# A one-layer decoder on one core: late SiLUs and biases moved into the last stage's fill, the opening re-ordered

## The reference, cut to what matters

```python
x = _layernorm(x + _L0_attn_ref(x, w_project, w_out))          # 16 heads of 16, causal
x = _layernorm(x + _L0_xattn_ref(x, ctx, Wq, bq, ..., bo))     # 8 heads of 8, rotary
x = _layernorm(x + _L0_ffn_ref(x, w1, b1, ln_g, ln_b, w2, b2))
# _L0_ffn_ref, with bitlinear158 = act_quant(rms_norm(x)) @ weight_quant(w).T + b
h = silu(bitlinear158(x, w1, b1))        # 256 -> 1024
h = gelu(h, approximate=False)
h = layer_norm(h, ln_g, ln_b)
return bitlinear158(h, w2, b2)           # 1024 -> 256
# rms_norm: x * rsqrt(mean(x*x) + 1e-5); act_quant: scale = 127 / max(max|x|, 1e-5) of each row
```

## Time and profile before

| | us |
|---|---|
| median of 3 runs | 517.94 |
| the three runs | 517.68, 519.66, 517.94 |
| the profiled execution, its own time | 520.89 |
| its span | 519.1 |
| busy: PE, DVE, ACT, POOL | 462.3, 427.4, 358.7, 308.3 |

### The profile page before, as it was taken

One profiled execution on the slowest core, in us unless ns is written; L12 is line 12 of the kernel. 1 busy time (PEld: TensorE's weight loads), 2 busy tenths in 40 slices (PEclk: granted clock), 3 DMA queues, 4 the chain that ended last, 5 costly groups with the idle time before them and its releaser, 6 DMA issues. The chain is left out here.

```text
span 519.1 us, 12269 instructions
## 1 busy us (share of the span) xinstructions
PE 462.3 (89%) x4294; PEld 245.2 (47%) x4294; DVE 427.4 (82%) x892; ACT 358.7 (69%) x689; POOL 308.3 (59%) x457
## 2 busy tenths in 40 slices
PE   6787889999999999999999999988998785977786
PEld 4454545455455455545545454543433232544453
DVE  2856687989889898798999999898786869799993
ACT  2232266678687786777878776676787876899973
POOL 6744556465474754657455677767453218688873
PEclk9998699999999999999999999999899897899999
DMA  7132323252442523324252332321100000000001
GB/s 225 32 90 73 93 57 102 59 159 63 121 128 68 147 63 99 114 59 147 60 141 69 105 101 62 102 58 54 32 3 1 0 1 2 10 29 24 32 30 42
DMA packets 52460, 37.07 MB, mean 71 GB/s; under 512 B 21552, under 2 KB 47792, under 8 KB 52400
## 3 DMA queue, kind: packets, MB, share of 16 engines
q1 hardware_dynamic: 52112, 36.06, 24.3%
q10 hardware_dynamic: 288, 0.23, 0.2%
HBM read 24.48 MB, written 10.49 MB: 67 GB/s over the span
## 5 line engine op out<-in xcount | busy, mean ns | idle before, releaser
L893 ACT ACTIVATE PB<-e_b 128x512 f32<-128x512 f32 x256 | 148.2, 592 | 59.9 <-PE e_b L690 58.8
L1087 DVE TENSOR_REDUCE MX<-mx_b 128x2 f32<-128x512 f32 x256 | 166.8, 679 | 26.2 <-PE mx_b L662 24.8
L662 PE MATMUL mx_b<-KA,QA 48*128 48x256 bf16 x512 | 98.5, 279 | 11.2 <-DVE MX L1087 10.7
L690 PE MATMUL e_b<-QA,KA 50*128 50x256 bf16 x512 | 97.5, 275 | 0.5 <-ACT PB L893 0.4
L707 PE MATMUL u_b<-PB,VA 128*32 128x256 f32 x1024 | 84.4, 393 | 2.1 <-ACT PB L893 1.7
L662 PEld LDWEIGHTS mx_b<-KA,QA 48*128 48x128 bf16 x512 | 29.7, 94 | 87.3 <-issue 48.3
L1014 POOL TENSOR_TENSOR SP<-SP,srec 128x1024 f32<-128x1024 f32 x15 | 28.5, 1901 | 68.2 <-DVE srec L1059 68.2
L1004 POOL TENSOR_TENSOR KM<-QK,att_tab 128x512 f32<-128x512 f32 x31 | 32.0, 1052 | 21.5 <-ACT QK L847 21.5
L567 PE MATMUL g_b<-XT,wp 128*128 128x128 f32 x256 | 34.5, 290 | 4.9 <-DMA wp<-in_wpT 4.9
L707 PEld LDWEIGHTS u_b<-PB,VA 128*32 128x32 f32 x1024 | 22.4, 108 | 31.2 <-ACT PB L893 16.8
L567 PEld LDWEIGHTS g_b<-XT,wp 128*128 128x128 f32 x256 | 31.5, 200 | 8.1 <-DMA wp<-in_wpT 4.9
(11 more groups left out here) (204 smaller groups left out, 1105.4 us busy)
## 6 DMA issues: line engine op xcount, KB each, us to landing
KA<-parts_k SPq DMA_DIRECT2D x64, 96.0 KB
QA<-parts_q SPq DMA_DIRECT2D x64, 96.0 KB
parts_q<-part_q SPq DMA_DIRECT2D x32, 128.0 KB, 1.9
parts_k<-part_k SPq DMA_DIRECT2D x16, 192.0 KB, 2.1
C<-in_ctx SPq DMA_DIRECT2D x16, 128.0 KB, 3.5
X<-in_x SPq DMA_DIRECT2D x16, 128.0 KB, 2.8
out_y<-O SPq DMA_DIRECT2D x16, 128.0 KB, 1.7
XT<-in_xT SPq DMA_DIRECT2D x15, 128.0 KB, 2.1
```

The source lines that it names most:

```text
L662: m = nc.tensor.matmul(mx_b[n % 2][:, D * k:D * k + D], QA[low:low + K_MAX, 2 * i.ring + b, h, P * u:P * u + P], KA[low:low + K_MAX, 2 * i ...
L690: m = nc.tensor.matmul(e_b[n % 2][:, D * k:D * k + D], KA[low:low + K_EXP, 2 * i.ring + b, h, P * sc:P * sc + P], QA[low:low + K_EXP, 2 * ...
L893: nc.scalar.activation(PB[:, n % 4].rearrange("p e t -> p (e t)"), e_b[n % 2][:, :], ACT.Exp, scale=XC ** -0.5).then_inc(e_sb.sem, 1)
L1087: nc.vector.tensor_reduce(MX[:, b, e, 2 * q:2 * q + 2, u], mx_b[n % 2][:, :].rearrange("p (e s) -> p e s", e=2), AXL.X, ALU.max).then_inc( ...
```

## The change

In the **opening** the first queries are split on GpSimd and no longer on VectorE; the second pair's scaling `self_norm` goes the other way; one pair of constant-row fills is put at VectorE's very start and one behind the second pair's norm on GpSimd; ScalarE copies the second pair's values ahead of its exponentials. In turn -1 the third pair's self-attention stands 4 steps earlier (sum at step 4, transposes at 8, value product at 9, projection at 11), and ten idle products are spread through it; eleven before it are taken out.

In the **last block** the SiLUs of pairs 12 to 15 and the biases of pairs 14 and 15 move behind the first GELUs (GELU of pairs 0 to 3 in one run, then a table load, SiLU 12, later SiLU 13 to 15, and a load back), the last pair's second norm is applied by GpSimd, the last two pairs have one group of factors and one batch, and GpSimd's upper product of the first pairs stands behind the roots as it did for the later ones.

```diff
-        GROUPS = (slice(0, NPAIR - 4), slice(NPAIR - 4, NPAIR - 2), slice(NPAIR - 2, NPAIR - 1), slice(NPAIR - 1, NPAIR))
-        BATCHES = (slice(0, 4), slice(4, 8), slice(8, 12), slice(12, 14), slice(14, 15), slice(15, 16))
+        GROUPS = (slice(0, NPAIR - 4), slice(NPAIR - 4, NPAIR - 2), slice(NPAIR - 2, NPAIR))
+        BATCHES = (slice(0, 4), slice(4, 8), slice(8, 12), slice(12, 14), slice(14, 16))
...
@@ TensorE, body and prologue
-                    if s == 12 and real(a):
+                    if s == (12 if i.v >= 0 else 8) and real(a):
                         transpose_p(a)
-                    if s == 13 and real(a):
+                    if s == (13 if i.v >= 0 else 9) and real(a):
                         self_pv(a)
...
-                    if s == 15 and real(a):
+                    if s == (15 if i.v >= 0 else 11) and real(a):
                         out_proj(a)
+                    if i.v < 0:
+                        idle_products({2: 1, 3: 1, 4: 1, 6: 2, 10: 1, 13: 1, 14: 1, 15: 1}.get(s, 0))
...
                 v_proj(p1, mx_b[0])
-                idle_products(4)
                 rotary_proj("q", mx_b[1], p0)
                 rotary_proj("k", e_b[1], p1)
                 qk_proj(p2, g_b[2])
-                idle_products(12)
+                idle_products(5)
                 transpose_p(p1)
@@ ScalarE, prologue and body
+                v_copy(p1, mx_b[0])
                 self_exp(p1, 1)
                 self_exp(p1, 0)
-                v_copy(p1, mx_b[0])
...
+                    if i.v < 0 and s == 8:
+                        pt_copy(a)
+                        ao_copy(a)
...
@@ VectorE
+            ones_rows(nc.vector, 1)
             dve.wait_ge(ld_att, 16)
...
-                    if s == 9 and real(a):
+                    if s == (9 if i.v >= 0 else 4) and real(a):
                         self_sum(a)
...
-                    if s == 6 and i.v in (NPAIR - 3, NPAIR - 1):
-                        factors(dve, i.v // (NPAIR - 1))
+                    if s in (5, 6, 7, 8) and i.v in (NPAIR - 3, NPAIR - 1):
+                        factor(dve, i.v // (NPAIR - 1), s - 5)
...
-                ones_rows(nc.vector, 1)
                 norm1_stats(p0)
...
                 rotate("q", mx_b[1], p0)
-                split_parts(dve, nc.vector, "q", p0)
                 self_sum(p1)
+                self_norm(dve, nc.vector, p1)
                 rotate("k", e_b[1], p1)
@@ GpSimd, prologue and body
-                wait(pool, km[1], p1, 1)
-                ones_rows(nc.gpsimd, 2)
-                pool.wait_ge(s_pad[2], 2)
                 rstd(pool, ln1, p0, mv1, rs1)
-                self_norm(pool, nc.gpsimd, p1)
+                split_parts(pool, nc.gpsimd, "q", p0)
...
+                if i.v < 0:
+                    wait(pool, ln1, j, 6)
+                    ones_rows(nc.gpsimd, 2)
+                    pool.wait_ge(s_pad[2], 2)
+                    self_norm(pool, nc.gpsimd, a)
                 if real(j):
                     split_parts(pool, nc.gpsimd, "q", j)
...
@@ last block, ScalarE
+        LATE, AHEAD_G = NPAIR - 4, 4
...
-            for v in range(NPAIR):
+            for v in range(LATE):
                 first_value(v)
...
-                if v == 4:
-                    norm2(act, last)
+                if v == 3:
                     square_sum(act, last)
-                if v == 7:
+                if v == 9:
                     numbers_copy(act, 4, t_b[1])
-                if v == 11:
-                    numbers_copy(act, 5, t_b[0])
+
+            for v in range(AHEAD_G):
+                second_value(Pair(0, v))
             for t in range(TURNS2):
                 second_values(t)
+                if t == 2:
+                    first_value(LATE)
+                if t == 3:
+                    for v in range(LATE + 1, NPAIR):
+                        first_value(v)
@@ last block, GpSimd
-                if i and t < FILL:
-                    upper_product(i)
...
-                if i and i.v != NPAIR - 1 and t >= FILL:
+                if i and i.v != NPAIR - 1:
                     upper_product(i)
...
-            mean_power(pool, 2)
             add_row(pool, 12)
             add_row(pool, 13)
             rstd(pool, ln2, last, mv2, rs2)
+            wait(pool, ln2, last, 6)
+            nc.gpsimd.tensor_scalar(XALL[:, last.v, :], Y2[:], rs2[:, 1:2], rs2[:, 2:3], ALU.mult, ALU.add).then_inc(ln2.sem, 1)
+            mean_power(pool, 2)
             quantise(pool, 14)
-            mean_power(pool, 3)
+            quantise(pool, 15)
...
@@ last block, TensorE
                 if i and i.v == 0:
+                    idle_sums(7, 0)
+                if i and i.v in (1, 2):
+
+                    pe.wait_ge(f_sb, f_done(NPAIR - 3 + i.v))
...
@@ last block, VectorE
-            for v in range(EARLY, NPAIR):
+            for v in range(EARLY, NPAIR - 2):
                 first_bias(v)
...
             for t in range(TURNS2):
                 (turn if t < DRAIN else drain)(t)
+                if t in (1, 2):
+
+                    first_bias(NPAIR - 3 + t)
```

More of the change, by code:

```diff
@@ L734, in early_product, with idle_products @@
                 m.then_inc(f_ps.sem, 1)
+            def idle_products(n):
+                for _ in range(n):
+                    nc.tensor.matmul(u_b[:, :], identb[:], maskb[:].rearrange("p h s -> p (h s)"), start=True, stop=True)
             pe.wait_ge(ld_wp, 16)
@@ L792, in body @@
                             pv_quad(i, m)
-            def idle_products(n):
-                for _ in range(n):
-                    nc.tensor.matmul(u_b[:, :], identb[:], maskb[:].rearrange("p h s -> p (h s)"), start=True, stop=True)
             def prologue():
@@ L1381, in second_values @@
                                          scale=root[:, (i.v + LAG_G) % 4, 0:1]).then_inc(zs.sem, 1)
-                if i := pair_at(t, 0):
-                    wait(act, silu, i, 1)
-                    nc.scalar.activation(row_h(i), row_h(i), ACT.Gelu).then_inc(gelu.sem, 1)
+                if (i := pair_at(t, 0)) and i.v >= AHEAD_G:
+                    second_value(i)
                 if j:
```

64 lines of the change are left out of this document (33 added, 31 removed).

## The result

The changed kernel took **506.27 us** (median, 504.90 to 512.86), the kernel before 518.48 beside it: ratio 0.9745, 95% interval [0.9719, 0.9771]. The forecast was 507.0. Six executions (one here, two of e1, one each of e6, e7 and e12) are over 1.5% longer than the fastest of their kernel: they count in the medians, but not in the ratios, the intervals and the clock means.

A forecast was written before the change was run, and what follows sets the result against it. Attention turns were taken as throughput-bound (TensorE 20.6 of 21.0 us), gains lying in the opening and last stage's start. -3.1 - 2.8 + 0.9 - 6.0 = -11.0 from 520.89, less 2.95, gave 506.9, said as 507.0; range 503.6 to 512.5.

The forecast's parts named there:

- Term 1: Opening: first maximum product moves from 44.07 to 41.0, set by the first queries' expansion; -3.1 us (bounds -4.3 and -1.5).
- Term 2: First maximum to first exponential product: 15.6 us instead of 18.41, VectorE's 12.7 the floor; -2.8 us (bounds 0 and -5.7).
- Term 3: First turn: second queries' expansion lands late (0.6) and third pair's norm starts later (0.3); +0.9 us (bounds 0 and +3).
- Term 4: Last stage's fill: first GELU 5.8 earlier, first square 6.4, third square 6.0 at low clock; -6.0 us (bounds -4 and -6.9).
- Rival 1: Opening gives almost nothing: terms two and three cancel and half of the first stays; 511.4 us, chance 0.2.
- Rival 2: Last stage: ScalarE pauses 1.3 us around each extra table load, all behind 2.6 late; 509.5 us, chance 0.1.
- Rival 3: Slower: fewer idle products, TensorE's clock stays low into the first turns; one whole low turn gives 527.5 us, chance 0.05.

The follow-up runs named there:

- e1: Kernel before with only the opening and turn -1 part of the change, last stage as before: 515.32 us, ratio 0.9931.
- e2: Kernel before with only the factors' groups and last-stage part of the change, opening as before: 512.19 us, ratio 0.9878.
- e6: Changed kernel with the four factor steps together at step 6 of turns 13 and 15, as before: 511.63 us, ratio 0.9785.
- e7: The changed kernel, unaltered, measured again beside the experiments: 509.74 us, ratio 0.9809.
- e12: Changed kernel with GpSimd's upper product ahead of the roots again in the last stage's first four turns: 509.87 us, ratio 0.9814.
- e10: Changed kernel with the first queries' split on VectorE again and the second pair's norm on GpSimd: 510.21 us, ratio 0.9845.
- e5: Changed kernel plus seven idle products before the first maximum product and idle sums before the second and third row sums: 505.66 us, ratio 0.9752.
- e9: e5 plus idle products in turn 13 and ahead of pairs 8, 10 and 11 in the last stage: 506.57 us, ratio 0.9763.
- e3: Changed kernel with the late SiLUs and biases ahead of the first GELU again, without the two extra table loads: 512.41 us, ratio 0.9893.
- e11: Changed kernel with pair 15's SiLU moved behind turn 6 of the last stage, adding two table loads: 513.37 us, ratio 0.9900.

## Why the prediction was right, and where not

**The number.** 507.0 was forecast, 506.27 and 509.74 were measured, the first 0.7 under it and the second 2.7 over. The range (503.6 to 512.5) held both. The nearness is in part luck. In the two profiles the gain was 15.05 us where the terms had 11.0; subtracting the 2.95 by which the profiled execution stood above its median made up for most of what the terms lacked, and the two medians of one kernel lie 3.5 us apart. The range's lower end, too, was not built from the terms' stated better ends: with -5.7 and 0 for terms 2 and 3, in place of -3.6 and +0.5, it is 501.0.

**Two readings of the rows.** The turn of 21.0 us was a window's width: from one copy of US to the next it is 21.91 us in both profiles for most turns. Nothing in the sum hung on it. And the page of before has an 8 in the slice from 363 to 376 us that the prediction passed over: it is the fall in turn 14 told below.

**Term 1 (-3.1; measured -3.28; by e10's profile 1.4 to 2.2 of it is the split's move).** The chain came as written: norm at 24.65 (25.4), sum at 27.48 (28.3), transposes at 30.30 (31.6), first maximum product at 40.79 (41.0), with TensorE waiting for the expanded queries. One split operation beside VectorE's scaling took 1.64 us, as in the earlier trace rows. The 1.3 us by which the transposes were early did not help, since the transfer decided: the step that took the transfer's distances from before is the one that carried the number. It did so with two errors that cancel: the split ended at 32.28 and not 33.1, and the queries landed 6.1 us behind the issue (34.68 to 40.79) and not 5.5 (34.87 to about 40.4 before). Over the profiles of this opening the product comes at 40.18 to 41.51.

**Term 2 (-2.8; -3.22 in the profile).** The placing gave 14.8 us at full clock; 14.38 was measured three times (e1, e5, e9). At low clock I had 16.5, and 17.7 to 20.7 were measured at 0.59 to 0.71. The mistake was to take VectorE's 12.7 us as the floor at any clock and to price the idle products as harmless: in e6, at 0.59, TensorE is busy 20.02 of 20.69 us and is itself the bound. Even the bound of 0 did not hold: that stretch is 2.3 us longer than before. That -3.22 came near -2.8 is a matter of which execution was profiled.

**Term 3 (+0.9; +0.27 in the profile, +0.9 in e5, +3.7 in e9).** The mechanism is the one named, the second queries' expansion landing late, where there is a wait to see: 0.69 us in e5, 2.10 in e9. In the changed kernel's own profiles, and in e6's, TensorE does not wait for it at all, and where their 0.27 comes from was not traced.

**Term 4 (-6.0; -7.63, by the medians of e2 -6.3).** First GELU -6.5 (from the stage's start; -5.8 forecast), first square -7.1 (-6.4), third -7.6 (-6.0). The first 0.7 us come from the first GELU, and e1 shows that they need not be an error of the placing: in the profile of before that GELU stands at 23.73, in e1, with the same last block and no fall of the clock in front, at 22.43. Against e1 the change brings it 5.2 us forward, less than forecast. The rest is the third row product: it started 0.8 us earlier and, though it ran at low clock as forecast (3.63 us), the path behind it was 0.8 us shorter than I had it. e3 shows that the late SiLUs and biases are most of this term (4.4 us by the ratios, with an error of 2.7; 6.4 of 7.6 at the third square). The interval of e2 is 3.6 to 9.1 us.

**What the sum lacked.** Turns 13 and 14, priced at nothing, gave 1.70 us in the profile: 0.55 from turn 13 and 1.15 from a fall of the clock that the profile of before had and that of after not. The second is an accident of the two executions profiled, since e7, the same kernel, has a larger fall there.

**How much is the clock.** The fit's constants, the time with no clock lost, are 511.5 for before and 503.7 and 505.4 for the two measurements of the changed kernel: 6 to 8 us are work and waiting. The clock lost went from 12.2 to 3.5 and 6.1 us, worth 5.3 and 3.7 us by the slope. I had treated the clock as a detail of two terms; by the fit it is four tenths of the gain, and about a third with the six long executions kept in. The fit is a correlation; what ties it to a cause is e5's filled gap in front of the first maximum product.

**The rivals.** Rival 1 (opening worth little, 511.4) lies outside e1's interval, though e1's 3.6 us stand between its 0.6 and my 5.0, and with the two longest executions in, the mean gain of 1.9 us is nearer to the rival. Rival 2 (a drain at each load) is refuted by the rows of e11: the Trainium skill, ScalarE: Activation LUTs, section "What ACT_TABLE_LOAD costs", has 1.38 us of drain, and no load here had one. Rival 3 (the clock falls and eats the gain) has half of its mechanism shown: falls of 3.5 to 17 us happen in the changed opening, but the kernel before has one of 13.7 too, and none reached far into the turns in a profile. It is not ruled out for single executions: one of e1's twelve, at a clock of 0.951, took 527.36 us, 8 more than the median of before. No profile shows where it lost its 25.7 us of clock.

## What to carry over

Where one execution's profile is compared with another's, compare the granted clock by place first: here 12 us of full clock were lost on average, in three or four stretches that come and go. Many of them follow idle times of TensorE of 1.2 to 3.4 us, but not all: the 13.7 us in the opening of before follow one of 0.95, and e1's 10.5 us near 366 one of 0.66. Idle products placed exactly where TensorE stands (here seven in front of a late transfer) went with a clock that held; spread over a stretch they did not hold it, and where it fell they probably cost time. Look at the longest executions as well as at the median: here they are the change's own. And before moving activations across a table load, look at what else waits for that engine: here a load was 1.28 us, and the wait that two loads and a SiLU passed on 2.25.

## What was not expected of the hardware

- The same program's granted clock differs by execution: the stretch after the first maximum product had 0.89, 0.71 and 0.59 in three profiles of one instruction order, at 15.20, 17.66 and 20.69 us, and 1.00 in a fourth, at 14.38.
- In turns 13 and 14 the clock fell in five of fourteen profiles, behind idle times of only 0.4 to 0.7 us each; the changed kernel's own two profiles, of one program, are one with the fall and one without.
- The second pair's expansion was issued 4.0 us behind the issue of its stores in e9 (50.82 to 54.84) and 2.75 in the changed kernel (50.30 to 53.05), with the same stores and maximum rows issued in between; TensorE then waited 2.10 us in e9 and not at all in the changed kernel. The stores themselves took 2.7 us to land in e9 and 1.9 in the changed kernel; why, no run shows.
